# A row-maximum pass split into 64x64 quarters of the array, with one ring of PSUM banks

## What is computed

```python
q, k, v = proj(layernorm(x), Wq, bq), proj(ctx, Wk, bk), proj(ctx, Wv, bv)   # 16 heads of 16
scores = einsum('bhqd,bhkd->bhqk', q, k) / sqrt(16)                          # 64 x 1601 per head
attn = softmax(scores, axis=-1)
x = x + einsum('bhqk,bhkd->bhqd', attn, v) @ Wo.T + bo
```

## Time and profile before

| what | value |
|---|---|
| runs, median | 717.5 us |
| profiled execution, first to last instruction | 715.7 us |
| between the two | 1.8 us |
| TensorE matmuls busy | 684.4 us |
| VectorE busy | 546.1 us |
| ScalarE busy | 450.0 us |
| GpSimd busy | 559.5 us |
| TensorE clock granted, mean | 0.988 |

### The profile page before, as it was taken

How to read it: one execution, slowest core, us unless ns; L and a number is a source line. 1 busy time by engine, 2 the same in 40 slices (tenths; PEclk the granted TensorE clock), 3 DMA queues, 4 the chain that set the end, 5 groups by cost and what they waited for, 6 DMA issues and landing times.

```text
span 715.7 us, 21609 instructions
## 1 busy us (share of the span) xinstructions
PE 684.4 (96%) x8681; PEld 511.2 (71%) x8681; DVE 546.1 (76%) x1135; ACT 450.0 (63%) x884; POOL 559.5 (78%) x378
## 2 busy tenths in 40 slices
PE   5889999999999999999999999999999998898898
PEld 2647776868776878687868786868686886666673
DVE  5598778868877887788768776887686986758757
ACT  2546766767666767676766666666666775655740
POOL 7996998899698969896989698869885797714122
PEclk9999999999999999999999999999999997999999
DMA  9586154544654454444444545454544330000223
GB/s 315 134 232 180 25 129 142 117 134 102 216 129 149 96 154 107 140 108 150 109 150 100 153 107 149 100 153 106 150 94 115 84 118 1 2 1 23 60 75 96
DMA packets 45434, 84.20 MB, mean 118 GB/s; under 512 B 8492, under 2 KB 28244, under 8 KB 45332
## 3 DMA queue, kind: packets, MB, share of 16 engines
q1 hardware_dynamic: 43720, 80.13, 40.9%
q0 software_dynamic: 912, 2.14, 1.0%
q10 hardware_dynamic: 704, 0.55, 0.3%
HBM read 36.89 MB, written 6.55 MB: 61 GB/s over the span
## 4 chain that ended last, share of the span: by engine, by line
PE 87%; DVE 5%; POOL 2%; issue 2%; ACT 1%; DMA 1%; SPq 1%; DVEq 0%; ACTq 0%; POOLq 0%
PE ps_kv L805 18%; PE ps_kv L796 17%; PE ps_score L856 12%; PE ps_front L828 12%; PE ps_out L880 11%; PE ps_score L904 2%; PE ps_kv L904 2%; PE ps_front L904 2%; PE ps_out L896 1%; PE ps_front L837 1%; DVE maxes L1486 1%; POOL clow L570 1%; DVE klow L1469 1%; PE ps_kv L771 1%; PE ps_front L890 1%
## 5 line engine op out<-in xcount | busy, mean ns | idle before, releaser
L627 POOL TENSOR_TENSOR plow<-prob 128x1024 bf16<-128x1024 f32 (+1 forms) x201 | 377.4, 1897 | 61.1 <-ACT prob L1224 58.6
L1486 DVE TENSOR_REDUCE maxes<-ps_front 128x1 f32<-128x512 f32 (+1 forms) x416 | 267.6, 664 | 68.2 <-PE ps_front L828 66.4
L1224 ACT ACTIVATE prob<-ps_score 128x512 f32<-128x512 f32 (+1 forms) x416 | 231.4, 596 | 47.4 <-PE ps_out L880 23.3
L856 PE MATMUL ps_score<-qstack,kstack 98*128 98x128 bf16 (+1 forms) x1664 | 141.5, 220 | 0.7 <-ACT prob L1224 0.4
L856 PEld LDWEIGHTS ps_score<-qstack,kstack 98*128 98x128 bf16 (+1 forms) x1664 | 111.9, 99 | 37.8 <-ACT prob L1224 1.5
L828 PE MATMUL ps_front<-kstack,qstack 96*128 96x512 bf16 (+1 forms) x512 | 135.5, 333 | 1.4 <-DMA kstack<-khigh 0.9
L880 PE MATMUL ps_out<-vstack,prob 128*128 128x65 bf16 (+1 forms) x1664 | 112.7, 194 | 0.6 <-DVE plow L1456 0.5
L1202 ACT ACTIVATE khigh<-ps_kv,bcol 128x512 bf16<-128x512 f32 (+1 forms) x123 | 72.9, 594 | 61.2 <-PE ps_kv L796 60.3
L805 PE MATMUL ps_kv<-w_hi,cbuf 128*128 128x256 bf16 (+1 forms) x402 | 109.9, 273 | 0.3 <-DVE vstack L1476 0.3
L805 PE MATMUL ps_kv<-w_hi,clow 128*128 128x256 bf16 (+1 forms) x402 | 109.7, 273 | 0.0
L805 PE MATMUL ps_kv<-w_lo,cbuf 128*128 128x256 bf16 (+1 forms) x402 | 109.7, 273 | 0.0
(11 more groups left out here) (288 smaller groups left out, 869.4 us busy)
## 6 DMA issues: line engine op xcount, KB each, us to landing
kstack<-khigh SPq DMA_DIRECT2D x256, 100.1 KB, 2.2
cbuf<-in_ctxT SPq DMA_DIRECT2D x15, 1601.0 KB, 7.1
kstack<-klow SPq DMA_DIRECT2D x128, 100.1 KB, 2.2
qstack<-q_blocks SPq DMA_DIRECT2D x48, 64.0 KB, 2.4
q_blocks<-qbd SPq DMA_DIRECT2D x16, 128.0 KB, 2.0
cbuf<-in_weT SPq DMA_DIRECT2D x2, 1024.0 KB, 7.2
slot_x<-att_all SPq DMA_DIRECT2D x1, 1024.0 KB, 10.7
vstack<-slot_x SPq DMA_DIRECT2D x4, 256.0 KB, 4.4
```

The lines of the kernel that those rows point to most:

```text
L627: nc.gpsimd.tensor_tensor(plow[slot][0:n, :], prob[slot][0:n, :], p_high(slot, 0, HP * P)[0:n], ALU.subtract).then_inc(plow_gps, 1)
L856: mm = nc.tensor.matmul(ps_score[0:nn, h % NSB, j * P:(j + 1) * P], kstack[par][0:98, hp, n0:n0 + nn], qstack[par][0:98, q_at(hp), :], sta ...
L1224: nc.scalar.activation(prob[slot][0:nn, e * 512:e * 512 + 512], ps_score[0:nn, h % NSB, :], ACT.Exp)\
L1486: nc.vector.reduce_max(maxes[:, hp:hp + len(unit), n], ps[:, 0:len(unit) * nn].rearrange("p (h k) -> p h k", k=nn), AX.X).then_inc(m_free, 1)
```

## The change

The two heads of a pair are kept in separate halves of the rows. `kstack` gets head one's 3 x 16 rows at 16 to 63, head two's at 64 to 111, each product's rows three apart, and rows 0 to 15 and 112 to 127 hold ones. In `qstack` those rows are zero, except that the shift now goes to rows 0 and 1 instead of 96 and 97 (a small DMA clears them before each maximum pass). A unit of the maximum pass then takes one piece of 512 keys of two pairs: four matmuls with 64 rows and 64 stationary columns, one on each quarter of the array, into two banks at once. There are 14 units per batch instead of 26, and one reduction reads both banks. `ps_front` and `ps_score` become one ring of four banks, given out in TensorE's order: two for a maximum unit, one for a score half or a shift (letter `R` now). All four programs are written anew, over all 16 batches. Line numbers of the changed kernel are other than before: L864 maximum pass, L892 scores, L916 weighing, L823 and L832 projections, L1526 reduction.

```diff
-                for at, hp, n in max_unit(m):
+                for at, pair, n in pieces:
                     n0, nn = piece(n)
-                    if n == 0:
-                        pe.wait_ge(k_stacked[hp], 48 * (b + 1))
-                    mm = nc.tensor.matmul(ps[:, at:at + nn], qstack[par][0:96, q_at(hp), :],
-                                          kstack[par][0:96, hp, n0:n0 + nn], start=True, stop=True)
+                    for j in range(2):
+                        rows = slice(64 * j, 64 * j + 64)
+                        for a in range(2):
+                            hp = 4 * half + 2 * pair + a
+                            if n == 0 and j == 0:
+                                pe.wait_ge(k_stacked[hp], STACKED * (b + 1))
+                                if hp == 0 and b < 2:
+                                    pe.wait_ge(ld_ones2 if b else ld_ones, 32)
+                            mm = nc.tensor.matmul(ps_ring[64 * a:64 * a + 64, place + j, at:at + nn],
+                                                  qstack[par][rows, q_at(hp), 64 * j:64 * j + 64],
+                                                  kstack[par][rows, hp, n0:n0 + nn], start=True, stop=True)
                 mm.then_inc(m_done, 1)
...
+def ring_plan():
+
+    at, before, held, place = {}, {}, [None] * RING, 0
+    count = dict.fromkeys("mRs", 0)
+    for letter in program(PE_PROGRAM):
+        if letter not in count:
+            continue
+        late = count["m"] == MUNITS * B and count["R"] == 2 * B
+        width = 2 if letter == "m" else 1
+        place = -(-place // width) * width % RING
+        if late and place < 2:
+            place = 2
+        unit = letter, count[letter]
+        banks = range(place, place + width)
+        at[unit], before[unit] = place, [held[n] for n in banks if held[n]]
...
-            sp.dma_start(kstack[0][96:98, :, :].rearrange("p a n -> p (a n)").bitcast(f32), ones2).then_inc(ld_ones, 16)
-            sp.dma_start(kstack[1][96:98, :, :].rearrange("p a n -> p (a n)").bitcast(f32), ones2).then_inc(ld_ones2, 16)
+            for par, loaded in ((0, ld_ones), (1, ld_ones2)):
+                for row in (0, P - DH):
+                    sp.dma_start(kstack[par][row:row + DH, :, :].rearrange("p a n -> p (a n)").bitcast(f32),
+                                 ones2[0, :].partition_broadcast(DH)).then_inc(loaded, 16)
...
+                sp.dma_start(qstack[par][0:2, :, :], qstack[par][2:4, :, :]).then_inc(q_loaded, 16)
...
-                nc.vector.reduce_max(maxes[:, hp:hp + len(unit), n],
-                                     ps[:, 0:len(unit) * nn].rearrange("p (h k) -> p h k", k=nn), AX.X).then_inc(m_free, 1)
+                width = len(pieces)
+                nc.vector.reduce_max(maxes[:, 4 * half + 2 * pair:4 * half + 2 * (pair + width), n]
+                                     .rearrange("p (x j) -> p j x", j=2),
+                                     ps_ring[:, place:place + 2, 0:width * nn].rearrange("p j (x k) -> p j x k", k=nn), AX.X)\
+                    .then_inc(m_free, 1)
```

The programs were one-batch strings repeated; a line of each of TensorE's:

```diff
-    ("KmmsswKmmsswwmKmmwKwwwwsKmKwssKsswwKmmsswwmKmmsswKwmswsKwmsmsKmmsswwmKmmsswwKmmsswKmmswwKmsmswwKmmsw"
+    "mKwwwwmmwwKRsKsssKmmKswwssswswsKsKmmKwswswwsssKmmKswswwssKmmwwsswwKwwmmwKwssRsKsKmmwwwKwmmwwKsRKsKs"
```

More of the change, by code:

```diff
@@ L155, in max_unit @@
 def max_unit(m):
-    half, nth = divmod(m, 4 * FULL + 1)
-    if nth < 4 * FULL:
-        return [(0, 4 * half + nth // FULL, nth % FULL)]
-    rest = SK - FULL * 512
-    return [(j * rest, 4 * half + j, FULL) for j in range(4)]
+    half, nth = divmod(m, HALF_UNITS)
+    if nth < 2 * FULL:
+        return half, [(0, nth // FULL, nth % FULL)]
+    return half, [(pair * (SK - FULL * 512), pair, FULL) for pair in range(2)]
 def q_at(hp):
     return 2 * (hp % 4) + hp // 4
-def front_pos(m):
-    return m + (m >= SHIFT_POS[0])
-FRONT = [m for m in range(MUNITS)]
-FRONT.insert(SHIFT_POS[0], MUNITS)
-FRONT.append(MUNITS + 1)
+def ring_plan():
[12 more added lines that the diff above has]
+        at[unit], before[unit] = place, [held[n] for n in banks if held[n]]
+        for n in banks:
+            held[n] = unit
+        place = (place + width) % RING
+        count[letter] += 1
+    return at, before
+RING_AT, RING_BEFORE = ring_plan()
+RING_LAST_S = max((n for (kind, n), place in RING_AT.items() if kind == "s" and place < 2), default=-1)
 BATCHES = range(B)
@@ L839, in shift_rows @@
+                for pair in range(2):
+                    for j in range(2):
+                        dst = ps_ring[0:98, place, :].rearrange("p (x a j q) -> p x a j q", x=2, a=2, j=2)[:, pair, :, j, :]
+                        mm = nc.tensor.matmul(dst, mparts[4 * half + 2 * pair + j],
+                                              ident_bf[:, :].rearrange("p (a q) -> p a q", a=2), start=True, stop=True)
                 mm.then_inc(shift_done, 1)
@@ L1091, in _ @@
             projections = iter([(b, u) for b in BATCHES for u in kv_order(b)])
-            fronts = iter([(b, m) for b in BATCHES for m in FRONT])
+            fronts = iter([(b, m) for b in BATCHES for m in range(MUNITS)])
+            shifts = iter([(b, half) for b in BATCHES for half in range(2)])
             scores = iter([(b, h) for b in BATCHES for h in range(2 * NCH)])
```

180 lines of the change are left out of this document (95 added, 85 removed).

## The result

The changed kernel takes 731.08 us, the median of four runs (729.45 to 732.46); the kernel before took 717.28 (716.03 to 718.16, four runs). The ratio is 1.0192, 95% interval 1.0166 to 1.0217: slower by 1.9%, where 707 and faster was forecast. The profiled execution has a span of 730.5 us, 14.8 more than before, and belongs to the run of 732.46.

What follows compares the result with a forecast made beforehand. The prediction took TensorE (PE), busy 96% of the span, as the bound until about 585 us. Its terms, -41.6 + 28.0 + 4 + 1 - 2 = -10.6 on 715.7, gave 705.1, with 1.8 more 706.9, rounded to 707; range 700 to 713.

Steps and rivals of the forecast that it cites:

- Term 1, columns: Maximum pass on TensorE: four quarters run in the time of one, -41.6 us, between -43.5 and -37.8.
- Rival 4: Maximum pass: bf16 quarters not fully four at a time, 749 at two at a time or 720; chance 0.06.
- Term 2, switches: Maximum pass: 112 runs going into quarters and back at 0.25 each, +28.0 us, between +21 and +38.
- Rival 1: Ways into quarters and back: each run costs the single-precision 0.34, time 717; chance 0.13.
- The 0.01 that the term takes off for smaller weights: Price per run of quarters: 0.26 lowered to 0.25 because bf16 weights of 64 columns are half the bytes.
- Term 3, waits on the ring: PSUM ring: TensorE waits for reductions to free banks, 0.04 per run, +4 us, from 0 to +15.
- rival 2: Ring: VectorE late with reductions holds PE, 0.12 per run more, +14, time 721; chance 0.15.
- PE's idle below 1 us in 100: Steady middle part: sign of a right forecast, TensorE idle less than 1 us in 100.
- Term 4, the start: Start: 1.54 MB more ones at 389 GB/s take 4.0 us, mostly hidden by projections; +1, from 0 to +4.
- Term 5, the tail: End of the kernel: PE's idle and slow-clock stretch get filled with work, -2 us, from 0 to -8.
- VectorE's total fell by 14.1 us: Whole kernel: sign of a right forecast, DVE busy at least 10 us less in total (0.6 per batch).
- the first L864 stands at 41.8: Start: sign of a wrong forecast, first maximum-pass matmul later than 33 us.

Runs made afterwards that it cites:

- experiment 8: Kernel before, with a tiny 16-column quarter matmul put ahead of each of its 384 full maximum units: 799.59 us, ratio 1.1117.
- experiment 10: Kernel of experiment 1, each reduction of the maximum pass reading only half of each piece of keys (output differs): 703.45 us, ratio 0.9807.
- Experiment 11: Kernel of experiment 1, only the last two of the seven units ahead of each shift reduced over half their keys: 708.38 us, ratio 0.9866.
- experiment 1: Changed kernel, rows of ones written by memsets and copies of GpSimd, VectorE and ScalarE instead of the four DMAs: 715.33 us, ratio 0.9954.
- experiment 2: Kernel before, its ones sent by four DMAs of 16 partitions instead of two of 2 partitions: 732.18 us, ratio 1.0178.
- experiment 5: Kernel before, with one more transfer, 1.54 MB of ones into 96 partitions, behind the two of ones: 726.09 us, ratio 1.0103.
- experiments 3 and 4: Changed kernel: 3 cuts its transfers of ones into 3.2 KB packets, 731.43 us; 4 gives each partition its own source row of memory, 732.55 us.
- experiment 6: Kernel before, with four more transfers of ones, each into sixteen partitions lying six apart: 727.22 us, ratio 1.0150.
- 7: Changed kernel, two of its four transfers of ones sent behind the first batch's stacks instead of ahead: 726.22 us, ratio 1.0108.
- Experiment 12: Kernel of experiment 1, with the shift one projection later in TensorE's order at 18 places: 728.08 us, ratio 1.0160.

## Why the prediction was wrong

**Term 1, columns: held.** A group of four bf16 quarters takes 0.22. The Trainium skill ("TensorE: Matmul & The Clock Gate", section "Measured speedup vs the span model") gives 3.07 for four row tiles; the quarters here, two by rows and two by columns, show 4. Rival 4 is out. The rest units take 0.06 and not the 0.12 assumed, so the term is nearer to its best bound, -43.5.

**Term 2, switches: held.** 0.10 on the way in, 0.13 inside and out, 0.24 in the mean of all starts, 0.213 when bought singly (experiment 8). 112 x 0.24 is +27 against +28.0. Rival 1 is out. The 0.01 that the term takes off for smaller weights is shown by no row or run.

**Term 3, waits on the ring: mis-sized.** The step said "I take 0.04 per run: +4, from 0 to +15". The traces show 0.9 to 1.0 us per batch, some +15 over 16 batches; experiment 10 gets 11.9 back by shorter reductions alone. It is the mechanism of rival 2, VectorE late on the ring, but mostly not at its place. I costed the score halves behind a pair of units, and L892 waits for `maxes` only three times with 1.5 us in all. The shift was not costed: its matmuls wait until VectorE has done the last two reductions and three small operations (L1542 is the last). Timeline of DVE, changed kernel, ahead of the shift that starts at 245.64:

```profile
242.89 0.74 DVE L1508 SCALAR_TENSOR_TENSOR klow<-ps_kv,bcol,khigh 128x512 bf16<-128x512 f32 x1
243.55 1.55 DVE L1526 TENSOR_REDUCE maxes<-ps_ring 128x2 f32<-128x1024 f32 x2
...
245.43 0.16 DVE L1542 TENSOR_REDUCE mwords<-mwords 128x4 f32<-128x8 f32 x1
```

The last pair of units is one of 1024 columns and the rest of 260. TensorE leaves it at 243.45, the chain ends at 245.59, and the two weighings and the projection between (1.8 us) cover all but 0.4 of it. What is behind the shift was not costed either: the second score half needs ScalarE's copy of it. Experiment 11 gives 7.0 of the 11.9 to the two units ahead of each shift. "PE's idle below 1 us in 100" came out at 1.36. That the reduction before the last in each half's chain had doubled was to be had from the order of VectorE shown in the section on the change; my count stopped at the fourth score half.

**Term 4, the start: wrong by the most.** It said "+1, from 0 to +4"; the measured cost is 15.7 (experiment 1) and 14.3 (experiment 2). Four steps failed. First, 1.54 MB were costed at the 389 GB/s of the earlier trace rows, but a rate belongs to its transfers: neighbours 0 to 15 and 112 to 127 took them at 126 GB/s (1.64 MB in 13.0 us), and well spread transfers of that kind at 229 (experiment 5). Second, the 3.9 us of projections placed ahead of the first maximum unit didn't hide it. The projections end at 30.4 in the changed kernel, and PE then waits for 11.4 us (the profile names no releaser, the stacks are what it waits for in the order); they are work that PE must do in any case, so they cover what is late only until they are used up. Without the transfers (experiment 1) they put the first unit 2.1 us later than before, at 30.67, not 3.9. Third, I looked at the stacks only, and not at what they wait for: `q_blocks` stands behind the ones, its landing is what SyncE waits for, and all 24 stack transfers of the batch come after it, at 0.6 us each. Fourth, the term had nothing for the clock: after the wait it was granted at 0.50 until 47 us, which cost some 1.8 us more (experiment 1). The lost time can't be had back, since PE was busy 99.8% in the part that follows.

The first of these was in the Trainium skill ("SBUF — State Buffer", section "Door 1: The DMA port swizzle"): the rate of a transfer goes by how many of SBUF's 16 DMA ports its partitions reach, and partitions 0 to 15 reach four, 104 GB/s for 1 MiB. By that page 1.64 MB take some 16 us, an estimate from its figure; the trace has 13.0. On neighbours the runs agree with it: neither source nor size of the packets counts (experiments 3 and 4), and sixteen partitions six apart go 1.76 times as fast (experiment 6). The page's table would let the 96 partitions of experiment 5, which reach all 16 ports, go faster than the 229 GB/s measured. The ports themselves no run here shows.

**Term 5, the tail: held** (-2, from 0 to -8), with 3.4 us won behind the fourteenth batch's first scores. Other traces with the same tail win more from there: 8.0 in experiment 1, 7.2 in 3, 5.9 in 4, 6.1 in 7; the trace of the result has one wait of 2.3 us for an exponential where experiment 1 has 0.4. Two more signs that the prediction named: VectorE's total fell by 14.1 us (at least 10 were expected), and the first L864 stands at 41.8 (later than 33 was to speak against term 4).

**The sum again**, with what was measured: -41.6 + 27 + 15 + 15.7 - 3.4 = +12.7, against 14.8 in the spans and 13.8 in the medians; 1 to 2 us have no term, about what is lost between the second batch and the sixth. Without the start's DMAs it is -3, and experiment 1 is 2.6 us faster than the kernel before: that is the version that beats both. But the agreement is partly luck. In its trace the fourteenth batch is still 4.1 us behind the kernel before, and all of the gain is made behind it, in the 8.0 us of the tail. With its start forecast rightly the change would still have been worth 2.6 us and not 11.6, and that rest is term 3. Left open: how far the waits at the shift can be taken away by another order. Experiment 12 shows that moving the shift alone makes it worse; no other order was run.

## What to carry to other kernels

Cost a transfer by the rate of transfers into the same partitions, never by a rate of other ones in a stretch nearby, and follow the queue: what stands behind it, who waits for that, and until when there is work to cover it. When units become fewer and larger, look at the end of each dependent chain, since a reduction there lies on the path in its new size. A saving in columns is only worth what the waits of the new order leave of it: measure it against the same order without the saving.

## What the runs showed of the hardware

- A transfer into sixteen neighbouring partitions: 3.24 us for a packet of 25.6 KB, 1.84 when the sixteen are six apart, 1.79 for two rows. All sixteen engines count as busy meanwhile (a share of 1.11 to 1.20 from 16 to 24 us), and two 128 KB transfers behind them in the queue take 17.9 and 19.0 us instead of 2.4 and 6.4.
- Going from the full array to quarters and back in bf16 costs 0.21 to 0.24 us, and four 64x64 quarters of bf16 run in the time of one full matmul (0.22 for 512 columns).
- After 11.4 us without work TensorE started again at 41.8 us at a granted clock of 0.50, its lower level of 1.2 GHz; it had 0.50 until 47 us and 1.00 from 48.
